# Two matrix products of a mixture of experts interleaved across lots, and its scatter and gather written out over eight buffers

## Chip, cores and metric

One NeuronCore of a Trainium2 chip runs the program; the other cores are idle. The metric is the device time of one execution in microseconds (us), here the median of three. The engines are PE (TensorE), DVE (VectorE), ACT (ScalarE), POOL (GpSimd) and SP (SyncE, which here only waits and starts transfers).

## The reference, cut to what matters

A graph network of two layers is followed by a mixture of experts over N = 6250 rows of D = 256; there are X = 8 experts with H = 1024 hidden units, and each row goes to two of them:

```python
gate_logits = xf @ Wg + bg
top_w, top_i = jax.lax.top_k(gate_logits, 2)
top_w = jax.nn.softmax(top_w, axis=-1)
for e in range(E):
    h = jax.nn.gelu(xf @ W1[e] + b1[e], approximate=False)
    out = out + w_dense[:, e:e + 1] * (h @ W2[e] + b2[e])
```

`xf` is the layer-normalised result of the graph network; the final output adds `out` to that result. The graph network takes the first 2.8 ms of the program and is not touched.

## The kernel before, in words

The experts' part has three stages, one after the other.

**Scatter.** The 49 tiles of 128 rows are normalised on DVE (`scatter_rows`, line 994) and POOL writes each tile twice into `lot_in` in DRAM by an indirect DMA (`scatter`, line 444), so that the rows of one expert lie together. Rows and indices go through two buffers (`xh`, `row_slot2`; `places`, line 990, copies the indices); the loop takes two tiles per iteration (`tile_loop`, line 263).

**Experts.** The rows of an expert are cut into lots of 256. How many lots an expert has is only known at run time (`lot_meta`: first lot and number of lots per expert), so every engine runs loops whose trip counts come from registers. For a lot, PE (lines 1232 to 1261) does eight *ups* (chunk c of the hidden units: six fp16 matmuls of 256 columns, since every operand is split into a high and a low part), four transposes of the next lot (`lot_transposes`, line 1225) and eight *downs* (again six matmuls each, accumulated over c in two banks). ACT (lines 599 to 612) takes each chunk through Gelu into `hid` (two buffers, line 610) and copies its high part to `hidT` (line 612); DVE (lines 1016 to 1028) computes the low part (line 1023). After the eighth low part DVE turns the next lot's transposes into high and low parts (`take_lot`, lines 1009 to 1014), and then takes the results out of PSUM (line 1028). `hidT` has one buffer, for all eight chunks of one lot.

What sets the order: PE may start the ups of lot n once `lotT_ready` says that take_lot(n) is done; an up of chunk c needs the Gelu of chunk c-4 done (four PSUM banks, `hid_sb`); the Gelu of chunk c needs the low part of chunk c-2 done (`hid_low`); a down of chunk c needs the low part of c.

The weights of an expert come as fp32 into one staging area, and POOL splits them into high and low parts (`split_expert`, line 421: two times two instructions at lines 427 and 428, then two at line 433) for one of two slots, even experts slot 0 and odd ones slot 1. The split of expert e waits for `expert_done` of e-2 (line 1261, given when the last down of e-2 is done) and for the load of its weights, which is issued after the split of e-1. SP (lines 339 to 345) loads the lots and stores the results.

**Gather back.** POOL fetches for every tile the two expert results by indirect DMA into `comb` (`gather_back`, line 466, two buffers), DVE adds them with their weights (`mix`, line 1034) and SP stores the tile. The gather of tile t waits for the mixing of tile t-2 and for the index copies that DVE does during the mixing of tile t-1.

Of the kernel before, what the change touches and what calls it, by code (L numbers as in the profile page):

```python
def build_program(nc, x, src, dst, edge_type, gnn_w, gnn_root, gnn_bias,
# [40 lines left out]
    HALVES = LOT // P  # L42
    LOTS = X + (2 * N) // LOT
# [25 lines left out]
    with ctx:  # L69
# [55 lines left out]
        lot_meta = sb("lot_meta", [1, X + 1, 2], i32)  # L125
# [49 lines left out]
        logits = carve(TILES, X)  # L175
        hidT = carve(KH * LOT).bitcast(f16).rearrange("p (a k c) -> p a k c", a=2, k=KH)
# [27 lines left out]
        comb = stage[:, 0:6 * D].rearrange("p (s c) -> p s c", s=6)  # L204
# [43 lines left out]
        scattered = [sem(f"scattered{s}") for s in range(2)]  # L248
# [3 lines left out]
        pos_ready = sem("pos_ready")  # L252
# [4 lines left out]
        back = [sem(f"back{s}") for s in range(2)]  # L257
        mixed1, mixed2 = sem("mixed1"), sem("mixed2")
        stored = [sem(f"stored{s}") for s in range(2)]
# [30 lines left out]
        def _(sp):  # L290
# [39 lines left out]
            for s in range(2):  # L330
                sp.wait_ge(scattered[s], 32 * (PAIRS + 1 - s))
# [16 lines left out]
            def store_out(t, i, s, first, last):  # L348
                sp.wait_ge(mixed2, t + 1)
                rows = LAST if last else P  # L350
                sp.dma_start(per_tile_dram(out, t, last), comb[0:rows, 4 + s, :]).then_inc(stored[s], 16)
            tile_loop(sp, store_out)
            sp.wait_ge(stored[0], 16 * (PAIRS + 1))
            sp.wait_ge(stored[1], 16 * PAIRS)
# [3 lines left out]
        def _(pool):  # L358
# [85 lines left out]
            def scatter(t, i, s, first, last):  # L444
                rows = LAST if last else P
                pool.wait_ge(zs_ready, t * 3 + 3)
                pool.sem_inc(gather_turns, 1)
                for k in range(2):
                    pool.indirect_dma_start(lot_in, bass.IndirectOffsetOnAxis(row_slot2[0:rows, s, k:k + 1], 0),
                                            xh[0:rows, s, :], None).then_inc(scattered[s], 16)  # L450
            tile_loop(pool, scatter)
# [14 lines left out]
            def gather_back(t, i, s, first, last):  # L466
                pool.wait_ge(pos_ready, t * 2 + 2)
                if not first:
                    pool.wait_ge(mixed2, t - 1)
                rows = LAST if last else P  # L470
                pool.sem_inc(gather_turns, 1)
                for k in range(2):
                    pool.indirect_dma_start(comb[0:rows, 2 * s + k, :], None, lot_out,  # L473
                                            bass.IndirectOffsetOnAxis(row_slot2[0:rows, s, k:k + 1], 0)).then_inc(back[s], 16)
            tile_loop(pool, gather_back)


        @block.scalar
        def _(act):
# [119 lines left out]
            with act.Fori(0, X) as e:  # L599
                act.load(regs, lot_meta[0:1, ds(e, 1), :])  # L600
# [15 lines left out]
        def _(v):  # L616
# [357 lines left out]
            v.tensor_copy(lot_meta[0:1, 0:X, 1], lots_f[0:1, 0, :])  # L974
            v.tensor_copy(lot_meta[0:1, X, 0:1], lots_f[0:1, 1, X - 1:X])
            v.tensor_tensor(rank, rank, run, ALU.add)
            link(v.memset(lot_meta[0:1, X, 1:2], 0))
# [12 lines left out]
            def places(t, s, signal):  # L990
                for k in range(2):
                    v.tensor_copy(row_slot2[:, s, k:k + 1], pos[:, k, ds(t, 1)]).then_inc(signal, 1)

            def scatter_rows(t, i, s, first, last):
                if not first:
                    v.wait_ge(scattered[s], i * 32)
                else:
                    v.wait_ge(zT_ps, TILES)
                normalise(t, s).then_inc(zs_ready, 1)
                places(t, s, zs_ready)  # L1000
            tile_loop(v, scatter_rows)


            regs2 = [v.alloc_register(f"dve_lots{i}") for i in range(2)]
# [4 lines left out]
            def take_lot(n):  # L1009
# [4 lines left out]
                v.scalar_tensor_tensor(lotT[:, 1], lot_psum, 2.0 ** Z_BITS, lotT[:, 0], ALU.mult, ALU.subtract).then_inc(lotT_ready, 1)  # L1014
            take_lot(0)
            with v.Fori(0, X) as e:
                v.load(regs2, lot_meta[0:1, ds(e, 1), :])
                start = v.snap(regs2[0], min_val=0, max_val=LOTS)
                lots = v.snap(regs2[1], min_val=1, max_val=LOTS)
                with v.Fori(0, lots) as j:  # L1020
                    for c in range(KH):
                        v.wait_ge(hid_high, (start + j) * KH + (c + 1))
                        v.scalar_tensor_tensor(hidT[:, 1, c, :], hid[:, c % 2, :], scales[:, 2:3], hidT[:, 0, c, :], ALU.mult, ALU.subtract).then_inc(hid_low, 1)  # L1023
                    take_lot(start + j + 1)
                    v.wait_ge(res_free, start + j + 1)
                    for h in range(HALVES):
                        v.wait_ge(res_ps, (start + j) * HALVES + (HALVES + h + 1))
                        v.scalar_tensor_tensor(lot_res[:, h, :], bank[2 + h][:, 0:D], undo[:, 1:2], down_bias_bc[:, ds(e * D, D)], ALU.mult, ALU.add).then_inc(res_sb, 1)


            for s in range(2):
                v.wait_ge(scattered[s], 32 * (PAIRS + 1 - s))

            def mix(t, i, s, first, last):
                if not last:
                    places(t + 1, 1 - s, pos_ready)
                rows = LAST if last else P
                here = acc[0:rows, ds(t, 1), :].rearrange("p a d -> p (a d)")
                v.wait_ge(back[s], i * 32 + 32)
                if not first:  # L1040
                    v.wait_ge(stored[s], i * 16)
                v.scalar_tensor_tensor(comb[0:rows, 4 + s, :], comb[0:rows, 2 * s, :], w1[0:rows, ds(t, 1)], here, ALU.mult, ALU.add).then_inc(mixed1, 1)
                v.wait_ge(mixed1, t + 1)
                v.scalar_tensor_tensor(comb[0:rows, 4 + s, :], comb[0:rows, 2 * s + 1, :], w2[0:rows, ds(t, 1)], comb[0:rows, 4 + s, :], ALU.mult, ALU.add).then_inc(mixed2, 1)
            places(0, 0, pos_ready)
            tile_loop(v, mix)


        @block.tensor
        def _(pe):  # L1050
# [171 lines left out]
            regs2 = [pe.alloc_register(f"pe_lots{i}") for i in range(2)]  # L1222
            pe.sem_inc(res_ps, HALVES)

            def lot_transposes(n):
# [4 lines left out]
                ins.then_inc(lot_taken, 1)  # L1230
            lot_transposes(0)
            with pe.Fori(0, X // 2) as i:
                for slot in range(2):
                    e = i * 2 + slot
                    pe.load(regs2, lot_meta[0:1, ds(e, 1), :])
                    start = pe.snap(regs2[0], min_val=0, max_val=LOTS)
                    lots = pe.snap(regs2[1], min_val=1, max_val=LOTS)
                    with pe.Fori(0, lots) as j:
                        n = start + j
                        pe.wait_ge(expert_in, i * 4 + (2 * slot + 2))  # L1240
                        pe.wait_ge(lotT_ready, n + 1)
                        for c in range(KH):
                            pe.wait_ge(hid_sb, n * KH + (c + 1))
                            for k in range(KD):
                                for wp, zp in PART_PAIRS:
                                    ins = pe.matmul(hid_bank[c % 4], up_sb[slot][:, wp, k, c * P:(c + 1) * P], lotT[:, zp, k, :],  # L1246
                                                    start=k == 0 and (wp, zp) == PART_PAIRS[0], stop=k == KD - 1 and (wp, zp) == PART_PAIRS[-1])
                            ins.then_inc(hid_ps, 1)
                        lot_transposes(n + 1)
                        for c in range(KH):  # L1250
                            pe.wait_ge(hid_low, n * KH + (c + 3))
                            for h in range(HALVES):
# [5 lines left out]
                                if c == KH - 1:  # L1258
                                    ins.then_inc(res_ps, 1)
# [25 lines left out]
```

## Time and profile before

| what | value |
|---|---|
| runs | 3967.58, 3969.45, 3976.3 us, median 3969.45 us |
| the profiled execution | 3979.79 us, its span 3978.1 us |
| PE, ACT, DVE, POOL busy over the span | 62 %, 33 %, 46 %, 50 % |
| mean granted TensorE clock | 0.802 of full speed |
| scatter stage (first indirect DMA to first lot loaded) | 2961.12 to 3107.4 us |
| experts, 53 lots | 3110.09 to 3803.95 us |
| gather back and end | 3807.96 to 3978.1 us |

Times inside the program count from the span's start. The average shares say little: the three stages have different limits, so each is read by itself. "Idle before" an instruction is put down to what released it; "issue" is time in which the profile shows nothing that was waited for.

### The profile page before, as it was taken

To read this page: it belongs to the slowest core of one execution; us is meant where nothing else is said; L and a number is where in the kernel's file an instruction comes from. 1 tells how busy PE (TensorE), PEld (TensorE's weight loads), DVE (VectorE), ACT (ScalarE), POOL (GpSimd) and SP (SyncE) were. 2 spreads that over 40 slices of the span, in tenths; PEclk is the share of its full clock that TensorE was granted. 3 is DMA by queue.
4 is the path that set the end of the run, shared out by engine and by line. 5 is a ranking of instruction groups with operands and counts; after the bars stand their busy time and mean duration, and the time that the engine had idled before them with its cause. 6 is when DMAs were issued, how large, how long until landed. Compare 5 with 4: busy or idle time off the path is not lost.

```text
span 3978.1 us, 83604 instructions
## 1 busy us (share of the span) xinstructions
PE 2481.0 (62%) x19188; PEld 1827.9 (46%) x19189; DVE 1818.6 (46%) x4454; ACT 1320.5 (33%) x2446; POOL 1987.4 (50%) x1865
## 2 busy tenths in 40 slices
PE   0144566677777775445667778889440677989920
PEld 0011334445565663123444556677430465878820
DVE  4722333444455553222334445556751455565533
ACT  0000112233344442001222334455210455878810
POOL 1465555655554543665566666565446556030045
PEclk9755667888898997557788899999655788999965
DMA  4232433333332332222333333333112221111133
GB/s 145 74 108 83 131 90 89 100 97 92 95 96 87 93 91 71 83 85 86 94 94 98 100 100 101 103 107 106 63 42 92 66 74 58 60 41 46 47 97 110
DMA packets 183768, 347.64 MB, mean 87 GB/s; under 512 B 35636, under 2 KB 122128, under 8 KB 183480
## 3 DMA queue, kind: packets, MB, share of 16 engines
q0 software_dynamic: 90128, 249.15, 21.2%
q10 hardware_dynamic: 56076, 58.83, 4.7%
q1 hardware_dynamic: 37404, 38.19, 3.0%
q14 instruction: 141, 1.16, 0.1%
q8 instruction: 19, 0.31, 0.0%
HBM read 282.24 MB, written 63.78 MB: 87 GB/s over the span
## 4 chain that ended last, share of the span: by engine, by line
PE 42%; issue 29%; DVE 11%; DVEq 7%; another core or an unknown queue 3%; ACT 3%; DMA 2%; POOL 2%; ACTq 2%; SPq 0%; POOLq 0%; PEldq 0%
PE bank L1125 12%; PE sum_banks L1105 8%; PE sum_banks L1256 6%; PE sum_banks L1106 6%; PE sum_banks L1246 3%; PE bank L1246 3%; PE bank L1117 3%; DVEq L816 2%; DMA stage<-lot_out,row_slot 2%; DVE sel_more L816 2%; DVEq L813 2%; DVE sel L808 1%; DVE edge_work L1023 1%; DVEq L799 1%
## 5 line engine op out<-in xcount | busy, mean ns | idle before, releaser
L405 POOL DMA_INDIRECT ring<-table,row_tab x1568 | 1505.0, 960 | 1144.5 <-SPq L314 756.8
L1125 PE MATMUL bank<-weights,stage 128*128 128x256 f16 x5292 | 894.9, 295 | 51.8 <-ACT stage L516 41.0
L1125 PEld LDWEIGHTS bank<-weights,stage 128*128 128x128 f16 x5292 | 524.9, 105 | 204.3 <-issue 72.1
L1105 PE MATMUL sum_banks<-ring,sel_more 128*128 x780 | 253.7, 326 | 583.4 <-issue 416.0
L554 ACT ACTIVATE stage<-sum_banks,inv 128x256 f16<-128x256 f32 x784 | 327.3, 471 | 866.6 <-DVE inv L841 382.0
L1105 PE MATMUL sum_banks<-ring,sel 128*128 x1568 | 466.0, 297 | 191.9 <-issue 101.1
L808 DVE SCALAR_TENSOR_TENSOR sel<-lane,win_off,key_tab 128x256 f16<-128x256 f16 x792 | 349.4, 483 | 448.2 <-PE bank L1125 289.8
L516 ACT ACTIVATE stage<-bank 128x1024 f16<-128x1024 f16 x392 | 401.6, 1025 | 277.4 <-remote 194.0
L816 DVE TENSOR_SCALAR sel_more<-lane,win_off,key_tab 128x128 f16 x780 | 259.0, 333 | 471.5 <-issue 289.7
L1106 PE MATMUL sum_banks<-ring,sel 128*128 x1568 | 466.2, 298 | 8.1 <-issue 7.7
L1105 PEld LDWEIGHTS sum_banks<-ring,sel_more 128*128 x780 | 80.0, 103 | 769.0 <-issue 765.1
L1023 DVE SCALAR_TENSOR_TENSOR edge_work<-stage,scales,edge_work 128x256 f16<-128x256 f32 x424 | 272.1, 646 | 296.8 <-ACT edge_work L612 296.6
L851 DVE SCALAR_TENSOR_TENSOR stage<-sum_banks,inv,stage 128x256 f16<-128x256 f32 x784 | 348.3, 480 | 56.3 <-issue 40.0
L1256 PE MATMUL sum_banks<-weights,edge_work 128*128 128x256 f16 x2544 | 304.5, 280 | 35.0 <-DVE edge_work L1023 35.0
L552 ACT ACTIVATE stage<-sum_banks 128x256 f16<-128x256 f32 x196 | 75.1, 383 | 695.7 <-DVE inv L841 263.1
L1105 PEld LDWEIGHTS sum_banks<-ring,sel 128*128 128x128 f16 x1568 | 161.2, 103 | 309.3 <-issue 283.8
L1256 PEld LDWEIGHTS sum_banks<-weights,edge_work 128*128 128x128 f16 x2544 | 253.8, 101 | 75.9 <-DVE edge_work L1023 41.7
L1106 PE MATMUL sum_banks<-ring,sel_more 128*128 x780 | 271.7, 349 | 17.2 <-issue 17.0
L1117 PE MATMUL bank<-ident,stage 128*128 128x128 f16 x3136 | 274.4, 238 | 2.1 <-DVE stage L851 1.0
L473 POOL DMA_INDIRECT stage<-lot_out,row_slot x98 | 94.3, 963 | 335.0 <-SPq L345 269.0
L838 DVE TENSOR_SCALAR inv<-sum_banks 128x2 f32 (+1 forms) x196 | 31.3, 160 | 484.7 <-PE bank L1125 226.5
L1117 PEld LDWEIGHTS bank<-ident,stage 128*128 128x128 f16 x3136 | 238.5, 108 | 21.5 <-issue 3.6
(249 smaller groups left out, 2739.3 us busy)
## 6 DMA issues: line engine op xcount, KB each, us to landing
ring<-table,row_tab POOLq DMA_INDIRECT x1568
weights<-L_ffn_W ACTq DMA_DIRECT2D x96, 178.5 KB
stage<-L_ffn_W POOLq DMA_DIRECT2D x16, 1024.0 KB, 6.9
edge_work<-lot_in SPq DMA_DIRECT2D x55, 256.0 KB, 2.7
lot_out<-edge_work SPq DMA_DIRECT2D x53, 256.0 KB, 2.2
lot_in<-zero ACTq DMA_DIRECT2D x47, 256.0 KB
table<-edge_work ACTq DMA_DIRECT2D x7, 896.0 KB, 4.1
table<-edge_work ACTq DMA_DIRECT2D x49, 128.0 KB
```

The lines of the kernel that those rows point to most:

```text
L405: pool.indirect_dma_start(ring_rows[:, b % RING, 0:2 * D], None, tables[layer], bass.IndirectOffsetOnAxis(row_tab[:, b:b + 1], 0)).then_in ...
L516: act.activation(means[:, par, :, :, 2 * k * WIN:(2 * k + 2) * WIN].rearrange("p q r (v n) -> p v (q r) n", v=2), ps_turn[slot].rearrange( ...
L554: act.activation(mean16[:, slot, h, 0:D], ps_sum[slot][h][:, 0:D], ACT.Copy, scale=inv[:, ds(c * 2 + h, 1)]).then_inc(mean_high[layer], 1)
L808: return v.scalar_tensor_tensor(sel[:, slot, h], lane16[:].unsqueeze(1).to_broadcast([P, 2, P]), win_off[:, ds(w, 1)], key_tab[:, ds(lo, 2 ...
L816: v.tensor_scalar(flat(sel_more[:, ds(block & (RING - 1), 1), :]), lane16[:], win_off[:, ds(w, 1)], key_tab[:, ds(block, 1)], ALU.add, ALU ...
L851: v.scalar_tensor_tensor(mean16[:, slot, h, D:2 * D], ps_sum[slot][h][:, 0:D], inv[:, ds(c * 2 + h, 1)], mean16[:, slot, h, 0:D], ALU.mult ...
L1023: v.scalar_tensor_tensor(hidT[:, 1, c, :], hid[:, c % 2, :], scales[:, 2:3], hidT[:, 0, c, :], ALU.mult, ALU.subtract).then_inc(hid_low, 1)
L1105: pe.matmul(to[:, 0:D + 1], hot, flat(slot[:, :, D:2 * D + 1]), start=first, stop=last, skip_group_check=True)
L1106: return pe.matmul(to[:, 0:D], hot, flat(slot[:, :, 0:D]), start=False, stop=last, skip_group_check=True)
L1117: out = [pe.transpose(ps_turn[slot][:, (4 * h + q) * P:(4 * h + q + 1) * P], mean16[:, slot, h, q * P:(q + 1) * P], ident16[:]) for h in r ...
L1125: return [pe.matmul(ps_out[par], rows[:, xp * KD + k, :], w16[:, wp, k, r * D:(r + 1) * D], start=part == 0 and n == 0, stop=part == PARTS ...
L1256: ins = pe.matmul(bank[2 + h][:, 0:D], hidT[:, hp, c, h * P:(h + 1) * P], down_sb[slot][:, wp, c, :], start=c == 0 and (hp, wp) == PART_PA ...
```

## The change

It does four things. (1) The first product of a lot is interleaved with the second product of the lot before it: a *turn* of PE is ups 0 and 1 of lot n, then for every c up c+2 of lot n and down c of lot n-1, with the transposes of lot n+1 at c = 5. The last eight downs stand alone at the end. ACT waits before it copies chunk c into `hidT` until down c of the older lot has read it. DVE does take_lot(n+1) after the low part of chunk 5 (it was after chunk 7) and the older lot's results after that of chunk 6. `expert_done` of an expert is given after the first turn of the next one. (2) `lot_meta` gets two more columns. (3) The scatter is written out over 49 tiles, with eight row buffers in `edge_work` and the indices read from `pos` in place. (4) So is the gather back, with eight buffers in `weights`; the mixing adds into `acc`, and the output is stored from there.

```diff
+    SPOTS = 8
...
+        z_rows = edge_work[:, cursor_z:cursor_z + SPOTS * D].rearrange("p (s c) -> p s c", s=SPOTS)
+        comb = weights[:, 0:2 * SPOTS * D].rearrange("p (s k c) -> p s k c", s=SPOTS, k=2)
...
 @block.gpsimd
+            for t in range(TILES):
+                rows = LAST if t == TILES - 1 else P
+                pool.wait_ge(zs_ready, t + 1)
                 for k in range(2):
+                    pool.indirect_dma_start(lot_in, bass.IndirectOffsetOnAxis(pos[0:rows, k, t:t + 1], 0),
+                                            z_rows[0:rows, t % SPOTS, :], None).then_inc(scattered[t % SPOTS], 16)
...
+            for t in range(TILES):
+                rows = LAST if t == TILES - 1 else P
+                if t >= SPOTS:
+                    pool.wait_ge(mixed2, t - SPOTS + 1)
                 for k in range(2):
+                    pool.indirect_dma_start(comb[0:rows, t % SPOTS, k, :], None, lot_out,
+                                            bass.IndirectOffsetOnAxis(pos[0:rows, k, t:t + 1], 0)).then_inc(back[t % SPOTS], 16)
...
 @block.scalar
                     for c in range(KH):
-                        if c == 0:
-                            act.wait_ge(res_ps, (start + j) * HALVES + HALVES)
...
                         act.wait_ge(hid_sb, (start + j) * KH + (c + 5))
+                        act.sem_inc(act_turns, 1)
+                        if c < KH - 1:
+                            act.wait_ge(down_done, (start + j) * (KH - 1) + (c + 1))
+                        else:
+                            act.wait_ge(res_ps, (start + j) * HALVES + HALVES)
                         act.activation(hidT[:, 0, c, :], hid[:, c % 2, :], ACT.Copy, scale=scales[:, 2:3]).then_inc(hid_high, 1)
...
 @block.vector
+            def lot_turn(n, m, older):
+                for c in range(KH):
+                    v.wait_ge(hid_high, n * KH + (c + 1))
+                    v.scalar_tensor_tensor(hidT[:, 1, c, :], hid[:, c % 2, :], scales[:, 2:3], hidT[:, 0, c, :], ALU.mult, ALU.subtract).then_inc(hid_low, 1)
+                    if c == KH - 3:
+                        take_lot(n + 1)
+                    if c == KH - 2 and older is not None:
+                        results(m, older)
...
 @block.tensor
+            def lot_turn(n, slot, m, older):
+                pe.wait_ge(lotT_ready, n + 1)
+                for c in range(2):
+                    up(n, slot, c)
+                for c in range(KH):
+                    if c + 2 < KH:
+                        up(n, slot, c + 2)
+                    if c == KH - 3:
+                        lot_transposes(n + 1)
+                    if older is not None:
+                        down(m, older, c)
...
+            def expert_turns(i, slot, first):
+                start, older, rest = expert_lots(i * 2 + slot)
+                pe.wait_ge(expert_in, i * 4 + (2 * slot + 2))
+                lot_turn(start, slot, older, None if first else 1 - slot)
+                if not first:
+                    pe.wait_ge(res_ps, start * HALVES + HALVES)
+                    pe.sem_inc(expert_done, 1)
+                with pe.If(rest > 0):
+                    with pe.Fori(0, rest) as j:
+                        lot_turn(start + j + 1, slot, start + j, slot)
...
+            for c in range(KH):
+                down(last_lot, 1, c)
```

## Rows read from the trace of the kernel before

**Rows 1.** Stretches: us, PE, PEld, DVE, ACT, POOL busy (instructions), PEclk, DMA share, GB/s

```profile
3400.00:3500.00 100.00, 100.00 (x910) 87.78 (x909) 54.73 (x110) 84.34 (x165) 0.00 (x0) 1.00 0.15 48
3804.50:3973.00 168.50, 0.00 (x0) 0.00 (x0) 55.30 (x197) 0.00 (x0) 94.33 (x98) 0.51 0.38 115
```

**Rows 2.** A quiet lot in order of time: start, length, instruction, idle before

```profile
3261.48 1.48 PE L1246 MATMUL sum_banks<-edge_work,weights 128*128 128x256 f16 x12
...
3262.46 0.56 ACT L610 ACTIVATE stage<-sum_banks,edge_work,undo 128x256 f32<-128x256 f32 x1 [1.45 <-PE sum_banks L1246]
...
3263.06 0.51 ACT L612 ACTIVATE edge_work<-stage,scales 128x256 f16<-128x256 f32 x1
...
3263.60 0.48 DVE L1023 SCALAR_TENSOR_TENSOR edge_work<-stage,scales,edge_work 128x256 f16<-128x256 f32 x1 [1.34 <-ACT edge_work L612]
...
3266.73 0.60 PE L1229 MATMUL bank<-ident,edge_work 128*128 128x128 f32 x4
...
3267.17 5.40 PE L1256 MATMUL sum_banks<-weights,edge_work 128*128 128x256 f16 x48
...
3270.55 0.48 DVE L1023 SCALAR_TENSOR_TENSOR edge_work<-stage,scales,edge_work 128x256 f16<-128x256 f32 x1 [0.51 <-ACT edge_work L612]
...
3270.96 0.68 DVE L1012 TENSOR_SCALAR edge_work<-bank 128x512 f16<-128x512 f32 x1
3271.67 0.69 DVE L1014 SCALAR_TENSOR_TENSOR edge_work<-bank,edge_work 128x512 f16<-128x512 f32 x1
...
3272.50 1.48 PE L1246 MATMUL sum_banks<-edge_work,weights 128*128 128x256 f16 x12
```

**Rows 3.** PE over the experts: first ups of lots 0, 1, 5, 14, 28, 30, 52, last downs

```profile
3110.09 2.74 PE L1246 MATMUL sum_banks<-edge_work,weights 128*128 128x256 f16 x12 [1.60 <-DVE edge_work L1014]
...
3124.22 1.48 PE L1246 MATMUL sum_banks<-edge_work,weights 128*128 128x256 f16 x12 [1.42 <-issue]
...
3201.60 2.74 PE L1246 MATMUL sum_banks<-edge_work,weights 128*128 128x256 f16 x12 [11.53 <-POOL weights L433]
...
3336.72 2.74 PE L1246 MATMUL sum_banks<-edge_work,weights 128*128 128x256 f16 x12 [11.97 <-POOL weights L433]
...
3509.70 1.48 PE L1246 MATMUL sum_banks<-edge_work,weights 128*128 128x256 f16 x12 [1.82 <-issue]
...
3544.62 1.47 PE L1246 MATMUL sum_banks<-edge_work,weights 128*128 128x256 f16 x12
...
3792.86 1.48 PE L1246 MATMUL sum_banks<-edge_work,weights 128*128 128x256 f16 x12 [1.40 <-issue]
...
3798.55 5.40 PE L1256 MATMUL sum_banks<-weights,edge_work 128*128 128x256 f16 x48
```

**Rows 4.** DVE low parts beside one weight-splitting instruction of POOL, in order of time

```profile
3221.56 5.69 POOL L427 TENSOR_SCALAR weights<-stage,scales 128x2048 f16<-128x2048 f32 x1
...
3222.45 3.74 DVE L1023 SCALAR_TENSOR_TENSOR edge_work<-stage,scales,edge_work 128x256 f16<-128x256 f32 x2 [0.51 <-ACT edge_work L612]
...
3227.13 0.49 DVE L1023 SCALAR_TENSOR_TENSOR edge_work<-stage,scales,edge_work 128x256 f16<-128x256 f32 x1 [0.93 <-ACT edge_work L612]
3228.12 3.74 DVE L1023 SCALAR_TENSOR_TENSOR edge_work<-stage,scales,edge_work 128x256 f16<-128x256 f32 x2 [0.51 <-ACT edge_work L612]
```

**Rows 5.** POOL: first instruction of the splits of experts 5 and 6

```profile
3306.02 5.43 POOL L427 TENSOR_SCALAR weights<-stage,scales 128x2048 f16<-128x2048 f32 x1 [62.34 <-PEq L1261]
...
3345.83 5.43 POOL L427 TENSOR_SCALAR weights<-stage,scales 128x2048 f16<-128x2048 f32 x1 [6.90 <-DMA stage<-L_ffn_W]
```

**Rows 6.** Indirect DMAs, busy and idle by releaser; the first scatter; idle times of L405

```profile
L449 POOL DMA_INDIRECT lot_in<-stage,row_slot x98 | 95.7, 977 | 95.3 <-issue 90.7 <-DVE row_slot L992 4.6
...
2961.12 1.08 POOL L449 DMA_INDIRECT lot_in<-stage,row_slot  x1 [52.40 <-issue]
...
L473 POOL DMA_INDIRECT stage<-lot_out,row_slot x98 | 94.3, 963 | 335.0 <-SPq L345 269.0 <-DVE row_slot L992 38.1 <-issue 27.9
...
  issue: 320.3, 951
```

More of the change, by code:

```diff
@@ L988, in _ @@
             v.sem_inc(routed, 1)
[L990 to L1004, printed above, removed]
+            for t in range(TILES):
+                if t >= SPOTS:
+                    v.wait_ge(scattered[t % SPOTS], spots_after + 32 * (t // SPOTS))
+                v.tensor_scalar(z_rows[:, t % SPOTS, :], acc[:, t, :], mv[:, t, 0:1], mv[:, t, 1:2], ALU.subtract, ALU.mult).then_inc(zs_ready, 1)
+            regs2 = [v.alloc_register(f"dve_lots{i}") for i in range(4)]
             v.sem_inc(res_sb, HALVES)
@@ L1014, in take_lot @@
                 v.scalar_tensor_tensor(lotT[:, 1], lot_psum, 2.0 ** Z_BITS, lotT[:, 0], ALU.mult, ALU.subtract).then_inc(lotT_ready, 1)
-            take_lot(0)
[L1016 to L1028, printed above, removed]
@@ L1031, in _, with results @@
[L1031 to L1042, printed above, removed]
+            def results(n, e):
+                v.wait_ge(res_free, n + 1)
+                for h in range(HALVES):
+                    v.wait_ge(res_ps, n * HALVES + (HALVES + h + 1))
+                    v.scalar_tensor_tensor(lot_res[:, h, :], bank[2 + h][:, 0:D], undo[:, 1:2], down_bias_bc[:, ds(e * D, D)], ALU.mult, ALU.add).then_inc(res_sb, 1)
@@ new lines, in later_lots @@
+            def later_lots(start, rest, e):
+                with v.If(rest > 0):
+                    with v.Fori(0, rest) as j:
+                        lot_turn(start + j + 1, start + j, e)
+            take_lot(0)
+            start, older, rest = expert_lots(0)
+            lot_turn(0, None, None)
+            later_lots(start, rest, 0)
+            with v.Fori(0, X - 1) as e:
+                start, older, rest = expert_lots(e + 1)
+                lot_turn(start, older, e)
+                later_lots(start, rest, e + 1)
@@ L1043, in mix @@
+            v.load(regs2, lot_meta[0:1, X:X + 1, :])
+            results(v.snap(regs2[2], min_val=0, max_val=LOTS), X - 1)
+            for t in range(TILES):
+                rows = LAST if t == TILES - 1 else P
+                s = t % SPOTS
+                v.wait_ge(back[s], spots_after + 32 * (t // SPOTS + 1))
+                v.scalar_tensor_tensor(acc[0:rows, t, :], comb[0:rows, s, 0, :], w1[0:rows, t:t + 1], acc[0:rows, t, :], ALU.mult, ALU.add).then_inc(mixed1, 1)
                 v.wait_ge(mixed1, t + 1)
-                v.scalar_tensor_tensor(comb[0:rows, 4 + s, :], comb[0:rows, 2 * s + 1, :], w2[0:rows, ds(t, 1)], comb[0:rows, 4 + s, :], ALU.mult, ALU.add).then_inc(mixed2, 1)
@@ L1230, in lot_transposes, with up @@
                 ins.then_inc(lot_taken, 1)
+            pe.sem_inc(down_done, KH - 1)
+            def up(n, slot, c):
+                pe.wait_ge(hid_sb, n * KH + (c + 1))
+                for k in range(KD):
+                    for wp, zp in PART_PAIRS:
+                        ins = pe.matmul(hid_bank[c % 4], up_sb[slot][:, wp, k, c * P:(c + 1) * P], lotT[:, zp, k, :],
+                                        start=k == 0 and (wp, zp) == PART_PAIRS[0], stop=k == KD - 1 and (wp, zp) == PART_PAIRS[-1])
+                ins.then_inc(hid_ps, 1)
@@ new lines, in down @@
+            def down(n, slot, c):
+                pe.wait_ge(hid_low, n * KH + (c + 3))
+                for h in range(HALVES):
+                    if c == 0:
+                        pe.wait_ge(res_sb, n * HALVES + (h + 1))
+                    for hp, wp in PART_PAIRS:
+                        ins = pe.matmul(bank[2 + h][:, 0:D], hidT[:, hp, c, h * P:(h + 1) * P], down_sb[slot][:, wp, c, :],
+                                        start=c == 0 and (hp, wp) == PART_PAIRS[0], stop=c == KH - 1 and (hp, wp) == PART_PAIRS[-1])
+                    if c == KH - 1:
+                        ins.then_inc(res_ps, 1)
+                    elif h == HALVES - 1:
+                        ins.then_inc(down_done, 1)
@@ L1231, in _ @@
             lot_transposes(0)
-            with pe.Fori(0, X // 2) as i:
+            expert_turns(0, 0, True)
+            expert_turns(0, 1, False)
+            with pe.Fori(1, X // 2) as i:
                 for slot in range(2):
[L1234 to L1252, printed above, removed]
-                                if c == 0:
-                                    pe.wait_ge(res_sb, n * HALVES + (h + 1))
-                                for hp, wp in PART_PAIRS:
-                                    ins = pe.matmul(bank[2 + h][:, 0:D], hidT[:, hp, c, h * P:(h + 1) * P], down_sb[slot][:, wp, c, :],
-                                                    start=c == 0 and (hp, wp) == PART_PAIRS[0], stop=c == KH - 1 and (hp, wp) == PART_PAIRS[-1])
-                                if c == KH - 1:
-                                    ins.then_inc(res_ps, 1)
-                    pe.wait_ge(res_ps, (start + lots) * HALVES + HALVES)
-                    pe.sem_inc(expert_done, 1)
```

66 lines of the change are left out of this document (31 added, 35 removed).

## The prediction, made before the changed kernel was run

> **What bounds the kernel now.** I read the busy shares by stretch first, then the timelines of the three stages, then the idle times of POOL's indirect DMAs. In a stretch of lots with POOL idle PE is busy for all of it at the full 2.4 GHz clock [rows 1]. There is no idle TensorE to fill there. The timeline of one quiet lot [rows 2] says what sets its length. The 48 up matmuls take 3266.73 - 3261.48 = 5.25 us, that is 0.656 us for the six of a chunk; the transposes take 0.44 us; with as many downs PE needs 2 x 5.25 + 0.44 = 10.94 us. The next lot starts after 11.02 us, right behind take_lot: 0.14 us after the end of L1014. So in such a lot PE and the chain ups, Gelu, low parts, take_lot are equally long. Over the stage 53 lots take 3803.95 - 3110.09 = 693.9 us, or 13.1 each [rows 3]; 53 x 11.02 would be 584. The other 110 us are lots beside a split and two long waits for weights: lots 28 and 29, beside the split of expert 7, take 34.9 us together, and before lots 5 and 14 PE waits 11.5 and 12.0 us for POOL [rows 3]. From POOL's waits and the starts I read the lots per expert as 1, 3, 1, 8, 1, 14, 24, 1.
>
> **Scatter and gather: the gain.** POOL issues 98 indirect DMAs in each stage and is busy for 0.96 us of each. In the gather its idle time is 38.1 us for DVE's index copies and 27.9 us of issue (the 269 are the wait for the experts) [rows 6]: 66.0 us in 97 gaps. Written out, with indices in place and eight buffers, only the gap between two instructions is left. The graph layers' gathers (L405) are such code: 320.3 us over 951 unwaited gaps, 0.337 us each [rows 6], so 97 gaps cost 32.7 us, saving 33.3; if every gap were 0.30, the commonest value in that timeline, 36.9. I take 34.5. In the scatter 95.3 us of idle less the 52.4 ahead of the first [rows 6] are 42.9 us; the same sum saves 10.2 to 13.8. I take 11, less 0.5 for four more small DVE instructions ahead of `routed`. The cover is bandwidth: 19.3 MB in and out over 133 us are 145 GB/s, where the gather now runs at 115 GB/s and a DMA share of 0.38 [rows 1], so the share goes to about 0.48. The mixing of a tile, two DVE instructions of 0.5 us, stays under the 2.6 us of its two gathers. Index copies and the second buffer's waits leave with nothing behind them. **Sum: -45 us, bounds -51 and -43.**
>
> **A quiet turn: a new wait.** Chunk 5 of lot n is now copied into `hidT` only after down 5 of lot n-1, its low part comes after the copy, and take_lot(n+1) stands behind that low part on DVE. But down 5 is third from last on PE. From the start of the turn, with the prices of [rows 2]: eight ups, the transposes and six downs are 14 x 0.656 + 0.44 = 9.63 us. The six ups' matmuls reach ACT 0.98 us after their start, so 0.33 beyond the 0.656: copy 5 starts at 9.96. The low part follows a copy by 0.54 (10.50), take_lot follows a low part by 0.41 (10.91), the next up follows the start of take_lot by 1.54: **12.45 us**. PE has finished downs 6 and 7 at 10.94 and stands still for 1.5 us in every turn. Against 11.02 us before, and (3792.86 - 3544.62) / 22 = 11.28 in the lots of expert 6 [rows 3], that is 1.2 to 1.4 us more. The other waits have room: up 4 wants the Gelu of chunk 0 at 3.9 us and gets it near 2.2 (after the last copy of the older lot and the table load), and the lot after next is loaded about 2 us before its transposes. The loop's register work falls into the stall, so I add only 0.4 us where an expert ends.
>
> **A turn beside a split.** Under each splitting instruction of POOL one low part of DVE takes some 3.3 us instead of 0.48: the pairs at 3222.45 and 3228.12 last 3.74 us each, one per POOL instruction of 5.69 us, and three low parts get through in that time [rows 4]. The Trainium skill, "SBUF — State Buffer", section "Who interferes with whom", says that DVE with two SBUF inputs and a GpSimd instruction that reads SBUF exclude each other until the first is finished; a low part has two such inputs, take_lot and the results only one. The trace agrees in kind, but DVE is free 1.06 us before POOL's instruction ends, so the sums go by the rows. Eight low parts at three per 5.69 us are 15.2 us, and about 1 us of take_lot and results does not fit into the gaps: **16 us**, bounds 12.45 (all hidden) and 17.5 (as now, 34.9 / 2). The lead-in of a lot, in which DVE has nothing to do, is what goes.
>
> **The weights' chain: later.** `expert_done` of an expert with few lots now comes one turn into the next expert. A split takes 3336.72 - 3306.02 = 30.7 us [rows 3, 5], its load about 9 us behind the split before it. Step by step, before in brackets [rows 3]: turn 0 has no downs: 11 us less two low parts, plus 1 for a slow clock: turn 1 at 3120.1 (3124.2). Expert 0 is done at 3132, expert 2's weights at 3163. Turns 1, 2, 3 are 13.5, 16, 16: turn 4 at 3166. Its downs are over 11.3 us later, expert 3 is split by 3208.4: turn 5 at 3208.5 (3201.6). Turn 5 is 15, with 2.5 us for a slow clock, as 12 matmuls in 2.74 instead of 1.48 us show after the same wait; 6 and 7 are 16, 8 to 12 are 12.45: turn 13 at 3318.2. Expert 3 is done only behind that turn's downs, 3329.5, so expert 5's weights come at 3360.5: turn 14 at 3360.6 (3336.7). Turn 14 is 15, two of 16, eleven of 12.45: turn 28 at 3545.0 (3509.7). Then 12.45, two of 16, twenty-one of 12.45: turn 52 at 3851.3 (3792.9). Its downs, 1 us of issue and the last eight downs alone (5.4 us): the end at 3869.0 (3803.95). **Sum: +65 us**, by stretch +7, +17, +11, +23, +7; 48 of it are the stalls of 37 quiet turns, 13 the split of expert 5. Nothing covers these: PE is the stage's only path then.
>
> **The forecast.** +65 - 45 = +20 us: 3969.45 + 20 = **3989.5 us**. The profiled execution (3979.79 us) lies 10 us over the median of the runs, so its like would be near 4000. For the case itself I give 3972 to 4008: six full turns beside splits between 12.45 and 17.5 us make -21 to +9, the gains' bounds -6 to +2.
>
> **The rivals.** (1) *Faster: the turn stays PE-bound.* If take_lot(n+1) gets through within the 1.3 us of downs 6 and 7, a quiet turn is 11.1 us: 40 turns less 1.35 are -54, 3935.5 us. What decides is the path from down 5 to the next up, 2.82 us by my sum; the whole change breaks even at a quiet turn of 12.45 - 20 / 37 = 11.9. For it speaks that it moves take_lot forward by two low parts; against it the copy's wait in the diff. The Trainium skill, "Perfetto Trace Analysis", section "Optimization Strategy", says that interleaving regimes with different busiest engines may help. The trace speaks against that here: in both halves of a quiet lot PE is the busy one. 14 %. (2) *No change: the splits become cheap.* Downs of the older lot need nothing from DVE, so PE could run through a blocked low part; at 12.5 us per turn beside a split, with an earlier turn 4, -24: 3965 us. Against it DVE's three low parts per POOL instruction. 14 %. (3) *Slower still: TensorE's clock falls.* If every stall is followed by 12 matmuls in 2.74 instead of 1.48 us, 37 x 1.26 = +47: 4036. Against it: after 1.42 us of waiting lot 1 runs at 1.48 [rows 3]; only the long waits show 2.74. 8 %. (4) *The write-out brings half*, because transfers and not POOL's issue limit it: +22, 4012. 6 %.
>
> **How the numbers follow.** The forecast's own case has 58 %. A measurement of this kernel can tell about 0.2 %, 8 us. Faster by more: rival 1 and 3 of rival 2's 14, 0.17. Within: 11 of rival 2 and 4 of my case, 0.15. Slower: the rest, 0.68. The range leaves out rival 1 and most of rival 3, 20 %: 3957 to 4012.
>
> **What would show it.** In quiet turns, first ups 12.45 us apart with 1.5 us of PE idle, released by DVE L1014 or its successor; between splits beside PE, 16 us; the first up of lot 5 98.4 us behind that of lot 0 (91.5 before), that of lot 14 250.5 us behind it (226.6 before); POOL's indirect DMAs 1.25 to 1.3 us apart. Quiet turns under 11.9 us would make the forecast wrong, and so would a gather stage of over 150 us from its first DMA to the end (170.1 before, 135 expected).

## The result, and the profile after

Before 3968.51 us (four runs, 3963.76 to 3976.3), after 3992.07 us (3988.7 to 3997.8): ratio 1.0068, interval 1.0042 to 1.0094, so 23.6 us slower. The forecast was 3989.5 us.

The profiled execution of the changed kernel took 3988.7 us, its span 3984.4 us. In it the graph part, which nothing touched, happened to end 22.3 us earlier than in the profile before (first scatter at 2938.80 instead of 2961.12), so spans can't be set against each other; stages can:

| stage | before | after | difference | forecast |
|---|---|---|---|---|
| first scatter DMA to first lot's transposes | 146.3 | 132.3 | -14.0 | -10.5 |
| experts, first up to last downs | 693.9 | 773.8 | +79.9 | +65 |
| first gather DMA to the end | 170.1 | 133.0 | -37.1 | -34.5 |
| sum | | | +28.8 | +20 |

The difference by stage windows of after (us, then PE, PEld, DVE, ACT and POOL busy, PEclk, DMA share, GB/s): the experts, a stretch of quiet turns, and the gather.

```profile
3073.76:3855.00 781.24, 606.26 (x5300) 521.93 (x5300) 389.12 (x636) 489.55 (x952) 190.86 (x49) 0.93 0.15 50
3400.00:3520.00 120.00, 108.17 (x977) 95.06 (x975) 55.78 (x116) 89.54 (x176) 0.00 (x0) 1.00 0.13 42
3855.00:3984.00 129.00, 0.00 (x0) 0.00 (x0) 47.46 (x98) 0.00 (x0) 91.22 (x96) 0.50 0.48 147
```

PE has the same 5300 matmuls to do. In quiet turns it was busy for all of the stretch before [rows 1]; now it is for 108.17 of 120 us. The gather runs at 147 GB/s and a DMA share of 0.48 (115 and 0.38 in [rows 1]). POOL's indirect DMAs over the whole program, with busy time, then idle time by releaser, and the first scatter, the first transposes and the first gather:

```profile
L450 POOL DMA_INDIRECT lot_in<-edge_work x98 | 95.5, 975 | 82.1 <-DVE edge_work L998 52.5 <-issue 29.6
L472 POOL DMA_INDIRECT weights<-lot_out,edge_work x98 | 94.2, 961 | 318.9 <-SPq L349 289.3 <-issue 28.0 <-DVE acc L1053 1.5
...
2938.80 1.08 POOL L450 DMA_INDIRECT lot_in<-edge_work  x1 [52.47 <-DVE edge_work L998]
3071.05 1.12 PE L1236 MATMUL bank<-ident,edge_work 128*128 128x128 f32 x4 [142.21 <-DMA edge_work<-lot_in]
3851.42 1.08 POOL L472 DMA_INDIRECT weights<-lot_out,edge_work  x1 [289.31 <-SPq L349]
```

Less what stands ahead of the first, 29.6 us are left in the 97 gaps of either stage, 0.305 us each (all but 1.5 us of it issue); DVE's index copies, 38.1 us of [rows 6], are gone.

One quiet turn of after in order of time (start, length, instruction, idle before), which answers to [rows 2]:

```profile
3267.21 1.48 PE L1244 MATMUL sum_banks<-edge_work,weights 128*128 128x256 f16 x12 [1.23 <-DVE edge_work L1011]
...
3275.73 0.60 PE L1236 MATMUL bank<-ident,edge_work 128*128 128x128 f32 x4
3276.17 2.13 PE L1254 MATMUL sum_banks<-weights,edge_work 128*128 128x256 f16 x18
3277.02 0.51 ACT L613 ACTIVATE edge_work<-stage,scales 128x256 f16<-128x256 f32 x1 [0.78 <-PE sum_banks L1254]
3277.57 0.49 DVE L1021 SCALAR_TENSOR_TENSOR edge_work<-stage,scales,edge_work 128x256 f16<-128x256 f32 x1 [1.26 <-ACT edge_work L613]
3277.97 0.68 DVE L1009 TENSOR_SCALAR edge_work<-bank 128x512 f16<-128x512 f32 x1
3278.69 0.69 DVE L1011 SCALAR_TENSOR_TENSOR edge_work<-bank,edge_work 128x512 f16<-128x512 f32 x1
3279.53 1.48 PE L1244 MATMUL sum_banks<-edge_work,weights 128*128 128x256 f16 x12 [1.23 <-DVE edge_work L1011]
```

Read from the transposes on: PE runs downs 5, 6 and 7 in a row. ACT's copy of chunk 5 waits for down 5 (released by PE L1254), the low part for the copy, take_lot for its turn behind the low part, the next ups for take_lot. The next turn comes 12.32 us behind this one, 1.23 of them PE's idle time. The first ups of lots 0, 5, 14, 15, 16, 17, 29 and 30 and the last downs, which answer to [rows 3]:

```profile
3073.76 2.74 PE L1244 MATMUL sum_banks<-edge_work,weights 128*128 128x256 f16 x12 [1.59 <-DVE edge_work L1011]
3177.69 2.74 PE L1244 MATMUL sum_banks<-edge_work,weights 128*128 128x256 f16 x12 [30.59 <-POOL weights L435]
3333.49 2.74 PE L1244 MATMUL sum_banks<-edge_work,weights 128*128 128x256 f16 x12 [30.58 <-POOL weights L435]
3347.32 1.48 PE L1244 MATMUL sum_banks<-edge_work,weights 128*128 128x256 f16 x12 [1.23 <-DVE edge_work L1011]
3368.62 2.74 PE L1244 MATMUL sum_banks<-edge_work,weights 128*128 128x256 f16 x12 [7.35 <-DVE edge_work L1011]
...
3384.98 1.26 PE L1244 MATMUL sum_banks<-edge_work,weights 128*128 128x256 f16 x10 [1.37 <-DVE edge_work L1011]
...
3532.77 1.48 PE L1244 MATMUL sum_banks<-edge_work,weights 128*128 128x256 f16 x12 [1.23 <-DVE edge_work L1011]
3554.06 2.74 PE L1244 MATMUL sum_banks<-edge_work,weights 128*128 128x256 f16 x12 [7.35 <-DVE edge_work L1011]
...
3842.08 5.48 PE L1254 MATMUL sum_banks<-weights,edge_work 128*128 128x256 f16 x48 [1.93 <-DVE edge_work L1016]
```

Lot 5 starts 103.9 us behind lot 0, lot 14 259.7 us (forecast 98.4 and 250.5; before 91.5 and 226.6). The waits for POOL are 30.6 us each where they were 11.5 and 12.0. Lot 16, in the middle of a split, has waited 7.35 us: the place where the forecast was off. DVE and POOL just before it:

```profile
3357.34 5.44 POOL L429 TENSOR_SCALAR weights<-stage,scales 128x2048 f16<-128x2048 f32 x1
3357.39 4.33 DVE L1021 SCALAR_TENSOR_TENSOR edge_work<-stage,scales,edge_work 128x256 f16<-128x256 f32 x2 [1.09 <-ACT edge_work L613]
3361.52 0.57 ACT L606 ACTIVATE stage<-sum_banks,edge_work,undo 128x256 f32<-128x256 f32 x1 [3.01 <-DVE edge_work L1021]
3362.27 0.51 ACT L613 ACTIVATE edge_work<-stage,scales 128x256 f16<-128x256 f32 x1 [0.18 <-ACT stage L606]
3362.75 5.45 POOL L430 TENSOR_SCALAR stage<-stage,scales 128x2048 f32<-128x2048 f32 x1
3362.81 4.33 DVE L1021 SCALAR_TENSOR_TENSOR edge_work<-stage,scales,edge_work 128x256 f16<-128x256 f32 x2 [1.09 <-ACT edge_work L613]
```

Two low parts get through per POOL instruction, not three as in [rows 4]. DVE gets its turn 1.09 us after its last low part (0.93 before), 0.06 us after POOL has begun the next instruction. In [rows 4] the third low part started at 3227.13, just ahead of POOL's next.

### The profile page after: what moved, and what is told of

The parts are those of the page before. It is cut to its first block, busy times and chain, and to the rows that moved or that the text cites. A ratio compares the mean times of both kernels' runs of the same rounds, so it can differ in the third digit from the quotient of the medians.

```text
span 3984.4 us, 83292 instructions
## 1 busy us (share of the span) xinstructions
PE 2473.0 (62%) x19188; PEld 1835.7 (46%) x19189; DVE 1805.7 (45%) x4262; ACT 1319.1 (33%) x2446; POOL 1988.7 (50%) x1865
## 3 DMA queue, kind: packets, MB, share of 16 engines
q0 software_dynamic: 90128, 249.15, 20.8%
## 4 chain that ended last, share of the span: by engine, by line
PE 42%; issue 27%; DVE 12%; DVEq 6%; POOL 5%; ACT 3%; another core or an unknown queue 3%; ACTq 2%; DMA 1%; SPq 0%; POOLq 0%; PEldq 0%
PE bank L1132 12%; PE sum_banks L1112 8%; PE sum_banks L1113 6%; PE sum_banks L1254 5%; PE sum_banks L1244 3%; PE bank L1244 3%; PE bank L1124 3%; POOL lot_in L450 2%; DVEq L817 2%; POOL weights L472 2%; DVE sel_more L817 2%; DVEq L814 2%; DVE edge_work L1021 1%; DVE sel L809 1%
## 5 line engine op out<-in xcount | busy, mean ns | idle before, releaser
L1021 DVE SCALAR_TENSOR_TENSOR edge_work<-stage,scales,edge_work 128x256 f16<-128x256 f32 x424 | 287.5, 681 | 379.1 <-ACT edge_work L613 379.0
L1254 PE MATMUL sum_banks<-weights,edge_work 128*128 128x256 f16 x2544 | 330.9, 273 | 10.3 <-DVE edge_work L1016 10.3
L1244 PE MATMUL sum_banks<-edge_work,weights 128*128 128x256 f16 x1272 | 175.2, 284 | 154.9 <-DVE edge_work L1011 90.2
L1254 PEld LDWEIGHTS sum_banks<-weights,edge_work 128*128 128x128 f16 x2544 | 248.3, 98 | 43.2 <-DVE edge_work L1016 14.6
L613 ACT ACTIVATE edge_work<-stage,scales 128x256 f16<-128x256 f32 x424 | 216.4, 510 | 155.6 <-PE sum_banks L1254 126.0
L472 POOL DMA_INDIRECT weights<-lot_out,edge_work x98 | 94.2, 961 | 318.9 <-SPq L349 289.3
```

The lines of the kernel that those rows point to most:

```text
L1254: ins = pe.matmul(bank[2 + h][:, 0:D], hidT[:, hp, c, h * P:(h + 1) * P], down_sb[slot][:, wp, c, :], start=c == 0 and (hp, wp) == PART_PA ...
```

## The experiments

Their chips differ. The chips of the first four kernels and of the last pair run the kernel before in 3612.89 and 3615.18 us, the chip of the others in 3968.33, like that of the result. So each run is set against the kernel before on its own chip. The changed kernel stands at +34.9 us in the run shown first and at +23.6 in the result, 11 us apart, so medians taken across chips settle nothing under some 12 us. The stages in the traces agree better: the interleaved experts took 773.8 us in the result's profile and 772.3 to 772.6 in the traces of three other runs (the changed kernel again, 3 and 5). Smaller differences are read from them.

**The changed kernel again**, beside runs 5 to 7:

> The changed kernel itself, beside the kernel before on this chip, since the first four experiments ran on a chip whose graph layers take some 350 us less. If the parts add up it is 82.7 - 47.1 = 35.6 us slower than the kernel before; by the stages of the first profiles (+80, -14, -37) 28.7. Expected 29 to 36 us slower.

4003.26 against 3968.33 us, 1.0081 (1.0056 to 1.0106), +34.9. From the third turn on, each turn was within 0.12 us of the one in the result's profile.

**1. take_lot before low part 5** instead of behind it: does the order on DVE make the stall?

```diff
                 for c in range(KH):
+                    if c == KH - 3:
+                        take_lot(n + 1)
                     v.wait_ge(hid_high, n * KH + (c + 1))
                     v.scalar_tensor_tensor(hidT[:, 1, c, :], hid[:, c % 2, :], scales[:, 2:3], hidT[:, 0, c, :], ALU.mult, ALU.subtract).then_inc(hid_low, 1)
-                    if c == KH - 3:
-                        take_lot(n + 1)
```

> The changed kernel, with take_lot(n+1) of DVE one place earlier: ahead of the low part of chunk 5 instead of behind it, so that it no longer waits for down 5 of the older lot. Theory (the stall of a quiet turn is down 5, copy 5, low part 5, take_lot): the quiet turn falls from 12.32 to 11.05 to 11.15 us, PE's idle 1.23 us goes, 37 x 1.2 = 45 us; beside a split the 7.35 us waits for take_lot shrink too, another 10 to 20 us: 3925 to 3945 us, faster than the kernel before. Rival (the gap between turns is the loop's own register and branch work, or the copy's wait in general): the turn stays at 12.3 us and the time within 5 us of 3992.

3594.43 against 3612.89 us, 0.9949 (0.9933 to 0.9966), -18.5; against the changed kernel some -54 (its experts' stage takes 719.6 us, where that one's takes 773.8). Its timeline in a quiet turn:

```profile
2901.59 0.60 PE L1236 MATMUL bank<-ident,edge_work 128*128 128x128 f32 x4
2902.51 0.68 DVE L1009 TENSOR_SCALAR edge_work<-bank 128x512 f16<-128x512 f32 x1
2903.22 0.69 DVE L1011 SCALAR_TENSOR_TENSOR edge_work<-bank,edge_work 128x512 f16<-128x512 f32 x1
2904.06 1.48 PE L1244 MATMUL sum_banks<-edge_work,weights 128*128 128x256 f16 x12
...
2915.07 1.48 PE L1244 MATMUL sum_banks<-edge_work,weights 128*128 128x256 f16 x12
```

take_lot begins 0.92 us after the transposes instead of 2.24, the next ups stand without idle time, and the turn is 11.01 us. The stall was that one place in DVE's order. Turns beside a split, taken from transposes to transposes, stayed at 14.1 to 15.6 and 21.7 to 22.3 us (15.2 and 22.35 in the changed kernel): of the further 10 to 20 us that I had expected there, 4 came.

**2 and 3. Each half of the change alone**: the written-out scatter and gather with the experts of before, and the interleaved experts with the scatter and gather of before.

> The changed kernel's scatter and gather back with the experts' loops of the kernel before. Theory (the parts add up): scatter stage 14 us and gather stage 37 us shorter than before, the experts at 694 us as before: 3968.5 - 51 = 3917 us, within 6. Rival (part of the gain in the changed profile comes from the lighter memory traffic that the longer experts' stage leaves, or the first lots lose by it): less than 40 us, 3928 or more.

3565.8 us, 0.9876 (0.986 to 0.9893), -47.1, of the -51 expected.

> The kernel before with the changed kernel's interleaved experts alone; scatter and gather back over two buffers as before. Theory: the experts' stage is 774 us instead of 694, the rest as before: 3968.5 + 80 = 4048 us. Rival (the profiled execution overstates it): 4033 us, as the +65 of the prediction would give.

3695.58 us, 1.0225 (1.0208 to 1.0242), +82.7. The halves add: +35.6, against +34.9 for both. A gain of 47 us and a loss of 83 hide in a change of 0.7 %. By stages the write-out is worth 36.9 us in the gather (170.3 us in run 3, 133.4 in run 2), as in the result, but in the scatter only 7.5: the old scatter took 139.7 us in run 3, on its chip, not the 146.3 of the profile before. Why it varies stays open.

**4. Short splits.** POOL splits 64 of 2048 columns for experts 2 to 7, so most of their weights are left unsplit; everything else is as in the changed kernel.

```diff
-            def split_expert(e, s):
+            def split_expert(e, s, width=EW):
...
-                    half = slice(b * EW, (b + 1) * EW)
+                    half = slice(b * EW, b * EW + width)
```

> The changed kernel with the splits of experts 2 to 7 cut to 64 of 2048 columns (most of the weights are left unsplit, so the numbers computed are of stale weights); loads and semaphores stay. Theory (turns beside a split are long, 18.8 us, because a low part of DVE is blocked by POOL's instruction, and lots 5 and 14 wait for the split itself): all turns are 12.3 us, the two waits of 30.6 us nearly vanish, the experts' stage is 660 to 670 us instead of 774: 3880 to 3890 us. Rival (the long turns beside a split come from its load's traffic, not from the instructions): only the two waits go, about 3935 us, and turns of 17 to 21 us remain behind each load.

3552.28 us, 0.9834 (0.9814 to 0.9853), -60.6, or some 96 us below the changed kernel. Six of the eight turns that had been beside a split are 12.3 to 12.6 us. The turns of lots 6 and 15 take 18.1 and 15.7: in them PE waits 4.50 and 3.14 us for the load of the next lot. That load is issued 0.7 us behind the second load of an expert's weights, lands 0.2 us after it and takes 9.2 and 7.8 us, where it takes 2.8 in a quiet turn. This is the first of the two waits:

```profile
2829.25 1.12 PE L1236 MATMUL bank<-ident,edge_work 128*128 128x128 f32 x4 [4.50 <-DMA edge_work<-lot_in]
```

So the instructions make the long turns, as the theory had it, and the loads' traffic, the rival, can lengthen a turn as well. The splits, as contention and as waits together, cost the changed kernel about 96 us.

**5. No extra signal.** ACT's copy now follows the Gelu by 0.18 us (released by ACT itself), where it was 0.04 before [rows 2], and 0.06 us too late was what the low part missed. I took the signal that the change adds between the two for the reason.

```diff
-                        act.sem_inc(act_turns, 1)
```

> The changed kernel without ACT's act_turns signal between the two waits ahead of the copy. Theory: with the added signal and wait the copy starts 0.74 us after its Gelu instead of 0.60, so that in a turn beside a split the third low part comes 0.06 us behind the start of POOL's next instruction and is blocked: two low parts per POOL instruction instead of three. Without the signal it comes in time, a pair of turns beside a split falls from 37.5 to 33 to 35 us, 10 to 18 us in all. Rival (two per instruction follows from the copy's wait for the older lot's down, not from 0.14 us): no change over 3 us. The quiet turn stays 12.2 to 12.3 in both.

4003.22 us, no different from 4003.26 of the changed kernel beside it. The copy now follows the Gelu by 0.11 us beside a split, and three low parts got through under some POOL instructions. But the three turns around a split (from transposes to transposes) were 15.16, 20.2 to 20.8 and 13.3 us where they had been 15.17, 22.35 and 12.44: 1 us for each of three splits, nothing at the first. The theory fell as the price of the term: what costs is that low parts are blocked at all, not the 0.06 us.

**6. Gelu output in PSUM.** The low part then has one operand in SBUF. To have room, both halves of a lot's result share bank 2.

```diff
-        hid = stage[:, 2 * EW:2 * EW + 2 * LOT].rearrange("p (s c) -> p s c", s=2)
+        hid = [bank[b][:, 0:LOT] for b in (3, 7)]
+        res_bank = [bank[2][:, h * D:(h + 1) * D] for h in range(HALVES)]
```

In runs 6 and 7 the first matmul of each half has the start flag (it begins a new sum), and that of the second half makes the first half lose chunk 0's contribution. That this is what gets lost is inferred: runs 8 and 9, with one flag, leave nothing out. The instructions are the same in number and size.

> The changed kernel with the Gelu's output in two PSUM banks instead of SBUF (both halves of the results share a bank for that), so that a low part reads only one operand from SBUF. Theory (DVE with two SBUF inputs and a POOL instruction that reads SBUF exclude each other): no low part is stretched beside POOL, turns beside a split are as long as quiet ones, 12.3 to 12.6 us, 40 to 50 us less than the changed kernel. Rival (POOL's instruction slows all of DVE or SBUF in general): low parts stay at 3.4 us, change under 10 us.

3955.3 us, 0.996 (0.9939 to 0.9982), -48.0 against the changed kernel. The timeline beside a split:

```profile
3201.16 5.43 POOL L431 TENSOR_SCALAR stage<-stage,scales 128x2048 f32<-128x2048 f32 x1
3201.17 0.48 DVE L1022 SCALAR_TENSOR_TENSOR edge_work<-bank,scales,edge_work 128x256 f16<-128x256 f32 x1 [0.83 <-ACT edge_work L614]
3202.48 0.48 DVE L1022 SCALAR_TENSOR_TENSOR edge_work<-sum_banks,scales,edge_work 128x256 f16<-128x256 f32 x1 [0.82 <-ACT edge_work L614]
3203.79 0.48 DVE L1022 SCALAR_TENSOR_TENSOR edge_work<-bank,scales,edge_work 128x256 f16<-128x256 f32 x1 [0.83 <-ACT edge_work L614]
3205.10 0.48 DVE L1022 SCALAR_TENSOR_TENSOR edge_work<-sum_banks,scales,edge_work 128x256 f16<-128x256 f32 x1 [0.83 <-ACT edge_work L614]
```

Four low parts of 0.48 us under one POOL instruction, and every turn beside a split is 12.27 or 12.28 us, but for that of lot 3, at whose end PE waits 6.07 us for weights. The mean of all 424 low parts falls from 681 to 482 ns. The changed kernel says the same without any edit: its low parts (two SBUF operands) are stretched, the results (L1016: one from PSUM, one from SBUF) never, with shortest, median and longest in ns:

```profile
L1021 DVE SCALAR_TENSOR_TENSOR edge_work<-stage,scales,edge_work x424: 469/484/4349, 3077.0 to 3842.3; 128x256 f16<-128x256 f32 x142
L1016 DVE SCALAR_TENSOR_TENSOR edge_work<-sum_banks,undo,edge_work x106: 469/477/484, 3101.4 to 3847.7; 128x256 f32<-128x256 f32 x106
```

Four pairs of results start 0.24 us into a POOL instruction and take no longer. In the third of these, the low part behind the pair is stretched under the same instruction:

```profile
3372.65 0.86 DVE L1016 SCALAR_TENSOR_TENSOR edge_work<-sum_banks,undo,edge_work 128x256 f32<-128x256 f32 x2
3373.43 3.50 DVE L1021 SCALAR_TENSOR_TENSOR edge_work<-stage,scales,edge_work 128x256 f16<-128x256 f32 x1
```

That is what the Trainium skill says ("SBUF — State Buffer", "Who interferes with whom"): outside the two-port modes, a DVE instruction with at most one SBUF input does not contend with GpSimd. The other half of its rule, that the blocked one waits for the whole instruction, is not what the traces show: in the changed kernel DVE is free some 3.9 us into POOL's 5.44.

**7. The same in the kernel without interleaving** (run 2 with Gelu's output in PSUM, the same contribution left out):

> Scatter and gather back written out, the experts of the kernel before, and the Gelu's output in PSUM. Theory: lots beside a split fall from 17.5 to 11 to 11.5 us, 13 + 15 + 16 + 12 = 56 us less than the written-out kernel without this, 47 + 55 = 102 us less than the kernel before on the same chip. Rival: as in the run above, no more than 57 us less than the kernel before.

3864.99 us, 0.974 (0.97 to 0.978), -103.3. All lots take 10.91 to 10.93 us, but the first and last of an expert. So not all of the 56 us below run 2 is contention: lots far from any split also fell, from 11.03 and some 11.25 us in run 2, which is some 8 us in all.

**8 and 9. The two orders of the experts, both mended.** Both with Gelu's output in PSUM and one start flag for the shared bank, so that nothing is left out; run 8 is interleaved with take_lot as in run 1, run 9 is run 7.

```diff
-                                        start=c == 0 and (hp, wp) == PART_PAIRS[0], ...
+                                        start=c == 0 and h == 0 and (hp, wp) == PART_PAIRS[0], ...
```

> The changed kernel with both of its turn costs mended: take_lot(n+1) ahead of the low part of chunk 5, and the Gelu's output in PSUM; of the two halves of the results that share a bank only the first matmul now carries the start flag. Theory: every turn is 10.95 to 11.05 us, and what is left against the written-out kernel of the next run is the lateness of expert_done alone: waits of about 20, 44 and 43 us between turns where that one has 13, 37 and 31, and 5 us of last downs. Expected 30 to 40 us slower than the next run, 62 to 72 us faster than the kernel before. Rival (interleaving hides the lead-in of a lot and so gains once the stalls are gone): as fast as the next run or faster.

> Scatter and gather back written out, experts' loops of the kernel before, Gelu's output in PSUM, only the first matmul into the shared bank with the start flag. Expected as e7: 0.974 of the kernel before, 98 to 108 us less; all lots 10.92 us but where an expert ends.

Interleaved 3546.22 us, 0.981 (0.9793 to 0.9827), -69.0; not interleaved 3511.84 us, 0.9717 (0.9703 to 0.9731), -103.3. Turns are 10.91 to 10.93 us in both, but those at an expert's start or end and two of the interleaved one (12.9 and 12.7 us) in which PE waits 1.72 and 1.57 us for a lot's load (the store ahead of it, which runs beside a load of weights, takes 5 us instead of 2.2). What is left between them, 34.4 us, is the price of interleaving alone. The waits for a split (engine and what it waited for: sum, times, longest), of the interleaved one:

```profile
PE sum_banks L1245 <- POOL weights L436: 69.1, 3, 30.6
```

and of the other:

```profile
PE sum_banks L1232 <- POOL weights L436: 41.0, 2, 23.4
```

From the first to the last transposes the interleaved one takes 663.8 us and the other 634.3, 29.5 more; PE's waits for weights, whose split could start only a turn later, are 28.1 of that. Another 3.8 us come behind the last transposes (4.22 us from them to the last eight downs instead of 0.44): three downs of the older lot take 2.0, and then PE waits 1.65 us until DVE has taken the older lot's results out of the bank. Run 9 is the best version found: 2.8 % below the kernel before.

## Why the prediction was right

By its own steps:

- **Scatter and gather, -45 (bounds -51 and -43).** Right in kind, at the far bound: -51.1 by stages in the result's profiles, -47.1 alone (run 2), the 4 us between them being the scatter. The gap between two indirect DMAs is 0.305 us, the commonest value of the graph layers and not their mean of 0.337. The bandwidth forecast (145 GB/s, 0.48) was met at 147 and 0.48, so rival 4, the write-out bringing half, fell.
- **A quiet turn, 12.45 us.** 12.32 measured, with 1.23 us of PE idle, released by take_lot (L1011). The copy of chunk 5 starts 9.81 us into the turn, where the sum had 9.96; the steps behind it are as forecast. Run 1 shows the path: with take_lot ahead of the low part that waits for down 5, the turn is 11.01. Rival 1 is what run 1 is and the change is not.
- **A turn beside a split, 16 us (bounds 12.45 and 17.5).** The step that failed. Two of them take 21.3 + 16.4 = 37.7 us (first ups of lots 15 to 17), 18.8 each, outside the bounds. Interleaving was to hide part of the contention, and hid none: it costs 18.8 - 12.3 = 6.5 us per turn, and some 6.3 in the six full lots of before (17.3 against 11.0). "Three low parts get through" was a count from [rows 4] taken over to a turn in which ACT's copies come later; it is two, and eight low parts at two per 5.44 us are 21.8 us, near the 22.35 of the longer turn (from transposes to transposes). Also missed: the upper bound "as now" gave DVE no chance to do worse. Eight such turns make +22.6, less 4.8 for the quiet turns and some 3 spread over the others: the +15 by which the experts' stage is off.
- **The weights' chain, later.** The waits of 30.6 us are there, before lots 5 and 14; together PE waits 61.2 us for POOL, 23.5 before. The runs show the lateness by itself in the 28.1 us of longer waits between runs 8 and 9. Of run 3's loss of 82.7, the place of take_lot (54 us by run 1, 48 of it in the 37 quiet turns) and the lateness with the last downs (34) would make 88; the two were measured in different kernels, and 5 us of overlap stay unexplained.
- **Rival 2, cheap splits,** fell: it needs run 6's placement. **Rival 3, the clock:** after the short stalls the 12 matmuls take 1.48 us, as forecast; after the 7.35 us stalls of lots 16 and 30 they take 2.74, as they did after 11.5 in [rows 3]. All four long turns beside a split end so; in no quiet turn does rival 3 come true.
- **The sum.** Gain 6 us larger by stage, loss 15 larger, +28.8 in one profile, +23.6 and +34.9 in two sets of runs. The nearness of 3989.5 to 3992.07 is partly luck: the two misses have opposite signs, and the same comparison gave 11 us more on another chip. The sign and the order of the terms are not luck.

The section of the Trainium skill on optimization strategy ("Perfetto Trace Analysis") says that interleaving may help where the busiest engine changes. Here it was PE in both halves, and interleaving them cost 34 us even with its two faults mended.

## What to carry to other kernels

Here the engine that does both products had no idle time to fill in a quiet lot, and interleaving them gained nothing. So look for idle time first, stage by stage, and then at what stands in program order ahead of the input of the next turn: one low part that waits for late work of the older lot, ahead of take_lot in DVE's order, cost 1.3 us in each of 37 turns. A "done" signal moved one turn later delays whatever starts from it: here the splits, 28 us of longer waits between runs 8 and 9. If GpSimd reads SBUF beside VectorE, try one of VectorE's two operands in PSUM before rearranging anything: it was worth 48 to 56 us here, as much as the whole write-out of scatter and gather (47).

## What the runs showed of the hardware that was not expected

- A count of how many VectorE instructions get through beside a GpSimd instruction is not a constant: 3 per 5.69 us or 2 per 5.44 us. The next low part came 0.1 us ahead of POOL's next instruction in the one case and 0.06 us behind it in the other, and run 5, which moved it forward, got three through again in places.
- Chips differ: the kernel before took 3968 us where the result and runs 5 to 7 were made, and 3613 and 3615 us where the others were. Nearly all of it lies in the graph part (first scatter at 2955.5 us in the changed kernel run again, at 2606.4 us in run 1), and there in POOL's 1568 indirect DMAs, which wait 745.7 us for SP's queue in the one and 400.0 in the other; quiet lots and the gather (133 us) agree. Why stays open.
- Two accumulations can share one PSUM bank with a single start flag, on the first matmul of the bank, at no cost in time: the experts' stage took 637.2 us with two flags (run 7) and 637.4 with one (run 9).
- Quiet lots of experts 3 and 5 took 11.02 us before, those of expert 6 11.23; with Gelu's output in PSUM all are 10.92. What makes the difference was not tried.
